# A two-layer gated transformer block in a fixed plan of steps: GpSimd's maxima moved together, turns moved, empty steps put in

## The chip, the core and the metric

The kernel runs on one core of one Trainium2 chip. The metric is the device time of one execution in microseconds (us). Engines: PE (TensorE), DVE (VectorE), ACT (ScalarE), POOL (GpSimd) and SP (SyncE, which issues all DMAs here).

## The reference

Eight batches of 512 tokens with 512 features, a context of 64 rows per batch, four layers one after the other:

```python
x = x + tanh(g_xattn[0]) * linear_attention(layernorm(x), ctx)   # stage A: 16 heads, gate, Wq Wg Wkv Wo
x = x + tanh(g_ffn[0]) * (gelu(layernorm(x) @ W1 + b1) @ W2 + b2)   # stage F: hidden size 2048
x = x + tanh(g_xattn[1]) * softmax(layernorm(x) @ ctx.T, mask) @ ctx
x = x + tanh(g_ffn[1]) * experts(layernorm(x))   # stage E: router over 32, top 8 merged into 8 groups of 192
```

In linear_attention, q and k go through `x + 1 if x > 0 else exp(x)`, and sums of keys times values over the context stand for the scores.

## The kernel before, in words

**Numbers in halves.** Each float32 operand of the large products is scaled by a power of two and split into an f16 "hi" and the f16 rest "lo"; a product is three f16 passes. So every weight tile (128x512) is loaded (SP, L1029), reduced to its largest magnitude by DVE (step `wmax`, L1721), and, once the maximum over a whole matrix is known, split: ACT writes hi (`wsplit`, L1518), DVE writes lo (`wlo`, L1753). The maximum over partitions is POOL's `partition_all_reduce` (step `all`, L1132); `pow` turns it into a scale on DVE (L1659 and after).

**One plan.** `make_plan` writes one list of steps by hand. Each engine walks that list and issues its part of every step in list order, waiting on semaphores; so the list sets the order on each engine, and an engine that waits keeps all later steps of its own back.

**Stage A** (L308 to L452; about 20 to 390 us): keys and values of the context (`kvk`, `kvv`, sums `kvsum`, L1318), then per batch: `q` x4 and `gate` x4 (12 matmuls each, L1259), `numden` x4 (L1327), `att` x4 (a turn, L1278), `out` x4 (L1342). The next batch's x is normalised between them: `stat` (L1686), `rs` (POOL, L1128), `norm` (L1699, two buffers), `turn` (PE transposes into a bank, L1278; ACT copies hi, DVE subtracts lo, L1707). `q` of the next batch needs all four turns. `q` on DVE is L1854, its feature map's sum on POOL L1147; `att` on DVE is L1881, its lo part on POOL L1154 (`attlo`). Beside these, `some()` hands out weight work: one call of `weights` is up to a `wlo`, a `wmax`, a `wsplit` and the `wload`s that are then allowed. The loads have four places in SBUF, tile k takes place k % 4: SP's load of tile k waits until tile k - 4 has left it, by its `wmax` if it was only measured and by its `wlo` if it was split. Every batch ends with a store of x and a load of the next one into the same buffer (SP waits for the store).

**Stage F** (to about 1069 us): `up` and `down` alternate (12 matmuls each, L1259 and L1362). In the last batch the second attention and the router of batch 0 are done between them.

**Stage E** (96 passes s, twelve per batch): PE's steps of a pass are `p16`, `p45`, `p7`, `p23` (12, 12, 6, 12 matmuls of 256 columns, L1269) in banks 4, 5, 4, 6, and four parts of `dn` (3 matmuls, L1460). DVE adds up the banks (L2060; L2065; L2070, L2074; L2081), ACT applies silu, DVE and POOL multiply (`mix`, L2087, L1222), ACT and POOL split the result (`mhi`, L1649, L1228). Between the parts stand five slots per pass, calls of `apart()`: after `p16`, `dn` 0, `dn` 1, `dn` 2, `dn` 3. Each takes one task of `side`, the attention and the router of the batch after (list L, then scores, softmax, reads, list M, then router and gating; all their PE work shares bank 7), and one of `finer`, the last weights. `None` is a task that does nothing. Tasks named below: `scores` (L1377), `soft3` (DVE, L1978 is its last), `pturn`, `read` x4 (L1392; DVE adds to x, L1999), `mturn`, `router` (L1404), `rout4` (L2030), `rout5` (L2035 to L2048), `rturn` (L1413), `gsum` (then SP stores the group weights and loads them for `mix`). The weight forms: `fsplit` (ACT), `flo` (POOL, with four sums that end at L1186), `fhi` (ACT, L1599), `flo2` (POOL, L1191).

Of the kernel before, what the change touches and what calls it, by code (L numbers as in the profile page):

```python
# [14 lines left out]
NT = TOK // P  # L15
NC = D // P
# [50 lines left out]
N_O = 12  # L67
# [66 lines left out]
def make_plan():  # L134
# [119 lines left out]
    def second_tasks(i):  # L254

        ph, b = i

        def stats(ts):
# [17 lines left out]
        if ph == "L":  # L276
            return begin + [norm(0), norm(1), None, turn(0, 2), None, turn(1, 3), None, turn(2), None, turn(3), None]

# [10 lines left out]
        def step(kind):  # L289
            return lambda: add(kind, b)  # L290
        return begin + [norm(0), norm(2), None, turn(0, 1), None, turn(2, 3), None, *s0, turn(1), None, turn(3), None, None,
                        both(lambda: add("router", b, banks=1), s1[0]), both(step("rexp"), s1[1]),
# [77 lines left out]
    for j in range(NC):  # L370
        add("gate", 0, j, banks=1)
        norm()
        if j == 0:
            add("vmax")
            add("all", "v")
        if j == 2:
            add("pow", "v")
        weights(N_O)
    for t in range(4):
        add("kvsum", t, banks=4)  # L380
        if t < 2:
            norm()
    for t in range(NT):
        norm()
        add("numden", 0, t, banks=2)
        weights(N_O)
    add("tables")
    add("all", "b1")
    add("ctxmax")
    add("all", "c")  # L390
    late.append(lambda: add("pow", "c"))
# [12 lines left out]
    for b in range(1, NB):  # L404
        norms = ln_tasks(("A", b + 1) if b + 1 < NB else ("F", 0), apart=True)
        for j in range(NC):
            add("q", b, j, banks=1)
            add("att", b - 1, j, banks=1)
            if j > 0:
                add("attlo", b - 1, j - 1)  # L410
            some()
        for j in range(NC):
            add("gate", b, j, banks=1)
            if j == 0:
                add("attlo", b - 1, NT - 1)
            if b == NB - 1 and j > 0:
                add("numden", b, j - 1, banks=2)
            for _ in range(2 if j < 2 else 1):
                norms.pop(0)()
            some()  # L420
# [43 lines left out]
    def attention_tasks(b):  # L464
# [19 lines left out]
        def gsum():  # L484
            add("gsum", b, banks=1)
            if b == 0:
                add("gload", 0)
                add("gload", 1)
        ahead, one = [None] * (3 if b == 0 else 5 if b == 1 else 0), [None] * (b != 1)
        return [*ahead, *L[:2], split, *L[3:], lambda: add("scores", b, banks=1), None, step("sexp"), step("soft2"),  # L490
                step("soft3"), None, lambda: add("pturn", b, banks=1), None, None, *[read(t) for t in range(NT)], *M,
                *one, lambda: add("rturn", b, banks=1), *one, gsum]

# [51 lines left out]
    def finish_weights():  # L545
# [5 lines left out]
        for t in range(NR):  # L551
            k = (0, 22, 28)[t // 4] + t % 4
            put(k, "wsplit", W_OF["d", t])
            put(k + 1, "wlo", W_OF["d", t])
            if t >= 4:
                put((11, 19)[t // 4 - 1], "wload", W_OF["d", t])
        s0 = W_OF["s", 4 * Q_EARLY]
        for i in range(4):
            put(0 if i < 2 else 5, "wload", s0 + i)
        for i, k in ((0, 12), (2, 16)):  # L560
            put(k, "fsplit", s0 + i)
            put(k + 1, "flo", s0 + i)
            put(k + 1, "fsplit", s0 + i + 1)
            put(k + 2, "flo", s0 + i + 1)
            put(k + 3, "fhi", s0 + i + 1)
            put(k + 4, "flo2", s0 + i + 1)

# [35 lines left out]
    for s in range(total + 3):  # L603
        b, j = divmod(s, NR)
        if s < total:
            if j == 0 and b == 0:
                finer = finish_weights()
            if j == 0 and b + 1 < NB:
                assert not side
                side = attention_tasks(b + 1)  # L610
        if 1 <= s <= total:
# [1527 lines left out]
```

## Time and profile before

| | |
|---|---|
| median of 3 runs | 1862.5 us (1860.62 to 1862.56) |
| profiled execution: its time, its span | 1858.95 us, 1857.2 us |
| mean granted TensorE clock | 0.989 |
| PE busy | 1789.2 us, 96% of the span |
| DVE, ACT, POOL busy | 1152.2, 601.2, 648.1 us |

The span runs from the first to the last instruction; the time has some 1.75 us around it. PE is the engine with almost no idle time, so what is to be read is where its idle time lies, and what ended it.

### The profile page before, as it was taken

How to read it: one execution, taken by the hardware profiler on the slowest of the kernel's cores; microseconds unless marked ns; L12 is line 12 of the kernel's file. 1: busy time of each engine (PE TensorE's matmuls, PEld its weight loads, DVE VectorE, ACT ScalarE, POOL GpSimd, SP SyncE). 2: the span in 40 equal slices, each digit the busy share in tenths (PEclk: the TensorE clock that was granted, in tenths of full speed). 3: DMA queues.
4: the chain of work that ended last, by engine and by line, in shares of the span. 5: the costliest groups of instructions: out<-in, count | busy, mean ns of one | idle time of the engine just before them, and what ended most of it. 6: DMA issues, size and time to landing. Idle time of an engine off the chain costs nothing.

```text
span 1857.2 us, 29113 instructions
## 1 busy us (share of the span) xinstructions
PE 1789.2 (96%) x11224; PEld 1068.4 (58%) x11224; DVE 1152.2 (62%) x2332; ACT 601.2 (32%) x961; POOL 648.1 (35%) x603
## 2 busy tenths in 40 slices
PE   8789999999999999999999979999999999999999
PEld 3545555544444444444444466677777777777776
DVE  5677777754545455453435577868677776768554
ACT  3324534311111124431112354333333434333422
POOL 1122422312012046642010355353544445353633
PEclk9899999999999999999999999999999999999999
DMA  5123443343314223221301051111112121211111
GB/s 160 51 68 123 141 130 103 91 131 67 93 46 114 92 55 97 68 77 34 91 1 63 20 160 57 62 55 54 67 44 77 41 80 41 78 36 54 35 63 46
DMA packets 152620, 137.69 MB, mean 74 GB/s; under 512 B 79970, under 2 KB 96482, under 8 KB 152482
## 3 DMA queue, kind: packets, MB, share of 16 engines
q1 hardware_dynamic: 152482, 135.84, 24.2%
q8 instruction: 88, 1.44, 0.3%
q14 instruction: 50, 0.41, 0.1%
HBM read 103.17 MB, written 32.64 MB: 73 GB/s over the span
## 4 chain that ended last, share of the span: by engine, by line
PE 76%; DVE 11%; POOL 5%; ACT 3%; issue 3%; DMA 2%; SPq 0%; DVEq 0%; ACTq 0%; POOLq 0%
PE bank L1259 21%; PE bank L1269 19%; PE bank L1362 15%; PE bank L1460 10%; PE bank L1342 4%; PE bank L1278 3%; DVE arena L1686 2%; PE bank L1327 1%; PE bank L1308 1%; POOL arena L1216 1%; DVE arena L1753 1%; DVE arena L2087 1%; DVE arena L2081 1%; POOL arena L1222 1%; PE bank L1377 1%
## 5 line engine op out<-in xcount | busy, mean ns | idle before, releaser
L1259 PE MATMUL bank<-arena 128*128 128x512 f16 x2304 | 526.0, 380 | 4.7 <-DVE arena L1707 2.6
L1269 PE MATMUL bank<-arena 128*128 128x256 f16 x4032 | 503.7, 273 | 10.3 <-DVE arena L2060 6.1
L1269 PEld LDWEIGHTS bank<-arena 128*128 128x128 f16 x4032 | 393.0, 98 | 125.8 <-DVE arena L2060 7.6
L1259 PEld LDWEIGHTS bank<-arena 128*128 128x128 f16 x2304 | 225.6, 98 | 269.7 <-issue 3.5
L1362 PE MATMUL bank<-arena 128*128 128x512 f16 x1536 | 356.0, 382 | 3.4 <-DVE arena L1922 2.0
L1460 PE MATMUL bank<-arena 128*128 128x512 f16 x1152 | 310.7, 380 | 0.0
L1912 DVE TENSOR_SCALAR arena<-arena 128x512 f16<-128x512 f32 x128 | 81.6, 637 | 301.2 <-ACT arena L1564 300.8
L1362 PEld LDWEIGHTS bank<-arena 128*128 128x128 f16 x1536 | 150.9, 98 | 186.5 <-issue 4.4
L1564 ACT ACTIVATE arena<-bank,arena 128x512 f32<-128x512 f32 x128 | 99.2, 776 | 429.7 <-PE bank L1259 426.6
L1222 POOL TENSOR_TENSOR arena<-arena 128x512 f32<-128x512 f32 x96 | 121.8, 1269 | 295.9 <-DVE arena L2087 295.9
L1637 ACT ACTIVATE arena<-arena 128x512 f32<-128x512 f32 x96 | 69.3, 722 | 287.8 <-DVE arena L2081 287.7
L1460 PEld LDWEIGHTS bank<-arena 128*128 128x128 f16 x1152 | 112.7, 98 | 58.9 <-issue 0.6
L1128 POOL TENSOR_TENSOR arena<-arena 128x4 f32<-128x4 f32 x32 | 34.4, 1076 | 315.3 <-DVE arena L1691 293.8
L1228 POOL TENSOR_TENSOR arena<-arena 128x512 f16<-128x512 f32 x96 | 113.2, 1179 | 62.1 <-ACT arena L1649 62.1
L1914 DVE SCALAR_TENSOR_TENSOR arena<-arena 128x512 f16<-128x512 f32 x128 | 117.7, 920 | 4.6
L2087 DVE SCALAR_TENSOR_TENSOR arena<-arena 128x512 f32<-128x512 f32 x96 | 74.9, 781 | 54.0 <-ACT arena L1637 53.7
L1147 POOL TENSOR_TENSOR arena<-arena 128x512 f32<-128x512 f32 x32 | 41.9, 1309 | 151.3 <-ACT arena L1540 137.7
L1699 DVE TENSOR_SCALAR arena<-arena 128x512 f32<-128x512 f32 x128 | 81.6, 646 | 18.5 <-POOL arena L1128 18.2
L1278 PE MATMUL bank<-arena 128*128 128x128 f32 x528 | 80.4, 277 | 13.0 <-DVE arena L1699 11.0
L1686 DVE BATCH_NORM_STATS2 arena<-arena 128x6 f32<-128x512 f32 x128 | 85.9, 671 | 8.6 <-DMA arena<-x_after_attention 8.1
L1342 PE MATMUL bank<-arena 128*128 128x512 f16 x384 | 89.1, 384 | 0.0
L2081 DVE TENSOR_TENSOR arena<-bank,arena 128x512 f32<-128x512 f32 x96 | 66.0, 688 | 34.5 <-PE bank L1269 33.8
(188 smaller groups left out, 1841.9 us busy)
## 6 DMA issues: line engine op xcount, KB each, us to landing
arena<-in_L_ffn_proj SPq DMA_DIRECT2D x64, 256.0 KB, 2.7
arena<-group_weights SPq DMA_DIRECT2D x64, 256.0 KB, 3.1
x_after_attention<-arena SPq DMA_DIRECT2D x8, 1024.0 KB, 5.2
arena<-x_after_attention SPq DMA_DIRECT2D x8, 1024.0 KB, 5.6
x_after_ffn<-arena SPq DMA_DIRECT2D x8, 1024.0 KB, 4.3
arena<-x_after_ffn SPq DMA_DIRECT2D x8, 1024.0 KB, 6.5
arena<-group_weights SPq DMA_DIRECT2D x64, 128.0 KB, 2.8
arena<-in_L_ffn_gate_up_proj SPq DMA_DIRECT2D x80, 96.0 KB, 2.0
```

The costliest lines, as they stand in the source:

```text
L1222: e.tensor_tensor(prod_s[s % 2], gw_s[s % 2], prod_s[s % 2], ALU.mult).then_inc(mixed)
L1228: e.tensor_tensor(macth_s[s % 3][1][:, 0, :], prod_s[s % 2], macth_s[s % 3][0][:, 0, :], ALU.subtract).then_inc(m_lo)
L1259: m = e.matmul(bank[b][:, :], wT[l][:, c, tile * P:(tile + 1) * P], y[h][:, c, :], start=n == 0, stop=n == NPASS - 1)
L1269: m = e.matmul(out, forms_of[j // 2][l][:, c, f, (j % 2) * P:(j % 2 + 1) * P], y[h][:, c0 + c, col:col + HT], start=n == 0, stop=n == 2 * ...
L1278: m = e.transpose(block4(b)[:, c, :], src[:, c * P:(c + 1) * P], ident)
L1342: m = e.matmul(bank[k][:, :], aT[h][:, c, cols], woT[l][:, c, :], start=i == 0, stop=i == NPASS - 1)
L1362: m = e.matmul(bank[t][:, :], hv[h][:, 0, t * P:(t + 1) * P], w2T[l][:, j, :], start=j == 0 and i == 0, stop=j == NH - 1 and i == 2)
L1460: m = e.matmul(bank[t][:, :], hv[h][:, 0, t * P:(t + 1) * P], dnT[l][:, j, :], start=j == 0 and i == 0, stop=j == NR - 1 and i == 2)
L1564: e.activation(h_s[(n - 1) % 2], bank[bank_of[step, 0]][:, :], ACT.Gelu, bias=b1T[:, j:j + 1], scale=inv["1"]).then_inc(gelu)
L1686: e.bn_stats(stats[:, t, :], x[:, t, :]).then_inc(bn1)
L1914: e.scalar_tensor_tensor(out=hh[1][:, 0, :], in0=hs, scalar=sc["t1"], in1=hh[0][:, 0, :], op0=ALU.mult, op1=ALU.subtract).then_inc(h_lo)
L2087: e.scalar_tensor_tensor(out=prod_s[s % 2], in0=prod_s[s % 2], scalar=inv["up"], in1=gate_s[s % 2], op0=ALU.mult, op1=ALU.mult).then_inc(prod)
```

## The change

Four things. In stage A, `all` of v, of the context (c) and of b1 stand directly before `all` of o, after batch 1's `rs`; all four turns of batch 1 stand beside the `kvsum`s; `numden` of batch 0 stands after `q` 0 of batch 1, with `pow` v and `tables` there, and batch 0's `att` one step later; the weight tiles of o are split from there on. In stage F's last batch and in stage E the empty tasks are dealt out anew (batch 0: `gap` is empty, 5 ahead; batch 1: 8 ahead; one before read 3, two before `rturn` and one before `gsum` for all). The last weights' times in `finish_weights` are later. `side` may now run over into the next batch.

```diff
@@ second_tasks
+        gap = [None] if b > 0 else []
-            return begin + [norm(0), norm(1), None, turn(0, 2), None, turn(1, 3), None, turn(2), None, turn(3), None]
+            return begin + [norm(0), norm(1), None, turn(0, 2), *gap, turn(1, 3), *gap, turn(2), *gap, turn(3), None]
-        return begin + [norm(0), norm(2), None, turn(0, 1), None, turn(2, 3), None, *s0, turn(1), None, turn(3), None, None,
+        return begin + [norm(0), norm(2), None, turn(0, 1), *gap, turn(2, 3), None, *s0, turn(1), *gap, turn(3), None, None,
@@ make_plan, beside gate of batch 0
         if j == 0:
             add("vmax")
+        if j == 1:
+            add("ctxmax")
+        if j == NC - 1:
             add("all", "v")
-        if j == 2:
-            add("pow", "v")
+            add("all", "c")
+            add("all", "b1")
         weights(N_O)
     for t in range(4):
         add("kvsum", t, banks=4)
-        if t < 2:
-            norm()
-    for t in range(NT):
         norm()
-        add("numden", 0, t, banks=2)
-        weights(N_O)
-    add("tables")
-    add("all", "b1")
-    add("ctxmax")
-    add("all", "c")
+    norm(2)
...
             add("q", b, j, banks=1)
-            add("att", b - 1, j, banks=1)
-            if j > 0:
-                add("attlo", b - 1, j - 1)
+            if b == 1 and j == 0:
+                add("pow", "v")
+                for t in range(NT):
+                    add("numden", 0, t, banks=2)
+                add("tables")
+            if b > 1:
+                add("att", b - 1, j, banks=1)
+                if j > 0:
+                    add("attlo", b - 1, j - 1)
+            elif j > 0:
+                add("att", 0, j - 1, banks=1)
...
@@ attention_tasks
-        ahead, one = [None] * (3 if b == 0 else 5 if b == 1 else 0), [None] * (b != 1)
+        ahead = [None] * (5 if b == 0 else 8 if b == 1 else 0)
-                step("soft3"), None, lambda: add("pturn", b, banks=1), None, None, *[read(t) for t in range(NT)], *M,
-                *one, lambda: add("rturn", b, banks=1), *one, gsum]
+                step("soft3"), None, lambda: add("pturn", b, banks=1), None, None, read(0), read(1), read(2), None, read(3), *M,
+                None, None, lambda: add("rturn", b, banks=1), None, gsum]
@@ finish_weights
-            k = (0, 22, 28)[t // 4] + t % 4
+            k = (8, 27, 33)[t // 4] + t % 4
...
-            put(k + 3, "fhi", s0 + i + 1)
-            put(k + 4, "flo2", s0 + i + 1)
+            put(k + 6, "fhi", s0 + i + 1)
+            put(k + 8, "flo2", s0 + i + 1)
...
-                assert not side
-                side = attention_tasks(b + 1)
+                side += attention_tasks(b + 1)
```

The order on POOL from the feature map of batch 0 (L1147, after the change L1155) to that of batch 1; `ISA` ahead of another kind of instruction is a change of POOL's configuration. Before:

```order
L1147 TENSOR_TENSOR arena<-arena 128x512 x4
L1132 ISA
L1132 ISA arena<-arena 128x1
L1128 ISA
L1128 TENSOR_TENSOR arena<-arena 128x4
L1132 ISA
L1132 ISA arena<-arena 128x1 x3
```

After:

```order
L1155 TENSOR_TENSOR arena<-arena 128x512 x4
L1136 TENSOR_TENSOR arena<-arena 128x4
L1140 ISA
L1140 ISA arena<-arena 128x1 x4
L1155 ISA
L1155 TENSOR_TENSOR arena<-arena 128x512 x3
```

`rs` moved ahead of all maxima, and two of the changes of configuration are gone.

The order on DVE in batch 4 of stage A, from `q` 2: L1854 and L1881 (after the change L1862, L1889) are `q` and `att`, L1753 (L1761) is `wlo`, L1721 (L1729) `wmax`. Before:

```order
L1854 TENSOR_SCALAR arena<-bank 128x512
L1881 SCALAR_TENSOR_TENSOR arena<-arena,bank 128x512
L1753 SCALAR_TENSOR_TENSOR arena<-arena 128x512
L1854 TENSOR_SCALAR arena<-bank 128x512
L1881 SCALAR_TENSOR_TENSOR arena<-arena,bank 128x512
L1753 SCALAR_TENSOR_TENSOR arena<-arena 128x512
L1721 TENSOR_REDUCE arena<-arena 128x1
L1686 BN_STATS arena<-arena 128x6
```

After:

```order
L1761 SCALAR_TENSOR_TENSOR arena<-arena 128x512
L1729 TENSOR_REDUCE arena<-arena 128x1
L1862 TENSOR_SCALAR arena<-bank 128x512
L1889 SCALAR_TENSOR_TENSOR arena<-arena,bank 128x512
L1761 SCALAR_TENSOR_TENSOR arena<-arena 128x512
L1729 TENSOR_REDUCE arena<-arena 128x1
L1694 BN_STATS arena<-arena 128x6
```

Before, the `wlo` ahead of the one `wmax` is of tile 43 and the `wmax` of tile 44; after, the pairs are tiles 40 and 44, 41 and 45, and a third one follows behind the statistics, 42 and 46. The same pairs stand in batch 1 after the change, four of them, tiles 8 and 12 to 11 and 15; before there are none.

The order on DVE at the end of the router's work in stage E, batch 7: L2060, L2065, L2070 (L2068, L2073, L2078) are the sums of `p16`, `p45` and `p7`. Before:

```order
L2060 TENSOR_TENSOR arena<-bank,arena 128x256
L2030 SCALAR_TENSOR_TENSOR arena<-arena 128x128
L2035 TENSOR_REDUCE arena<-arena 128x4
L2037 RECIPROCAL arena<-arena 128x4
L2039 TENSOR_SCALAR arena<-arena 128x4
L2041 TENSOR_TENSOR arena<-arena 128x128
L2046 CAST arena<-arena 128x4x32
L2048 TENSOR_TENSOR arena<-arena 128x4x32
L2065 TENSOR_TENSOR arena<-bank,arena 128x256
L2070 TENSOR_TENSOR arena<-bank,arena 128x256
```

After:

```order
L2038 SCALAR_TENSOR_TENSOR arena<-arena 128x128
L2073 TENSOR_TENSOR arena<-bank,arena 128x256
L2043 TENSOR_REDUCE arena<-arena 128x4
L2045 RECIPROCAL arena<-arena 128x4
L2047 TENSOR_SCALAR arena<-arena 128x4
L2049 TENSOR_TENSOR arena<-arena 128x128
L2054 CAST arena<-arena 128x4x32
L2056 TENSOR_TENSOR arena<-arena 128x4x32
L2078 TENSOR_TENSOR arena<-bank,arena 128x256
```

`rout5` moved from ahead of `p45`'s sum to behind it, ahead of `p7`'s.

## Rows read from the trace of the kernel before

**Rows 1.** Windows: length, busy us (x instructions) by engine, PEclk, DMA share, GB/s.

```profile
989.50:997.20 7.70, 5.19 (x20) 2.47 (x19) 5.23 (x11) 1.37 (x2) 1.44 (x1) 0.78 0.20 51
```

**Rows 2.** PE's waits: us in total, times, longest.

```profile
PE bank L1413 <- DVE arena L2048: 11.3, 8, 2.5
```

**Rows 3.** Timeline of PE, stage A: start, us, what, [idle before <-releaser].

```profile
64.86 3.76 PE L1318 MATMUL bank<-arena 128*128 128x132 f32 x32
71.91 3.86 PE L1318 MATMUL bank<-arena 128*128 128x132 f32 x16 [3.29 <-DVE arena L1841]
...
121.24 1.12 PE L1278 MATMUL bank<-arena 128*128 128x128 f32 x4 [5.68 <-DVE arena L1699]
```

**Rows 4.** Timeline of POOL, stage A.

```profile
67.52 0.38 POOL L1132 PARTITION_ALL_REDUCE arena<-arena  x1 [5.84 <-issue]
...
106.11 1.25 POOL L1147 TENSOR_TENSOR arena<-arena 128x512 f32<-128x512 f32 x1 [6.81 <-issue]
```

**Rows 5.** Timeline of DVE, stage A: one `numden` and `tables`, start to next start.

```profile
83.11 0.35 DVE L1863 TENSOR_SCALAR arena<-bank,arena 128x8 f32<-128x8 f32 x2
...
84.46 0.14 DVE L1659 TENSOR_SCALAR arena<-arena 128x1 uint32<-128x1 uint32 x1
...
94.79 0.42 DVE L1811 CAST arena<-arena 128x512 f32<-128x512 uint8 x1
...
96.51 0.15 DVE L1846 TENSOR_REDUCE arena<-arena 128x1 f32<-128x16 f32 x1
```

**Rows 6.** DMA issues, stage A, two stretches: count, KB each, us to landing.

```profile
arena<-in_L_ffn_proj SPq DMA_DIRECT2D x1, 256.0 KB, 2.9
...
x_after_attention<-arena SPq DMA_DIRECT2D x1, 1024.0 KB, 5.3
```

**Rows 7.** Timeline of DVE, stage A, batch 4.

```profile
229.85 0.74 DVE L1753 SCALAR_TENSOR_TENSOR arena<-arena 128x512 f16<-128x512 f32 x1
...
236.33 1.00 DVE L1699 TENSOR_SCALAR arena<-arena 128x512 f32<-128x512 f32 x2 [0.55 <-POOL arena L1128]
```

**Rows 8.** Timeline of PE, stage A, batch 4.

```profile
237.77 0.60 PE L1278 MATMUL bank<-arena 128*128 128x128 f32 x4
```

**Rows 9.** Timeline of PE, end of stage F.

```profile
992.62 1.12 PE L1278 MATMUL bank<-arena 128*128 128x128 f32 x4 [2.51 <-DVE arena L1699]
...
1005.28 1.56 PE L1377 MATMUL bank<-arena 128*128 128x64 f16 x48 [1.46 <-DVE arena L1707]
...
1046.41 1.41 PE L1404 MATMUL bank<-arena 128*128 128x32 f16 x48 [1.91 <-ACT arena L1564]
...
1058.39 0.38 PE L1413 MATMUL bank<-arena 128*128 128x128 f16 x4 [1.53 <-DVE arena L2048]
```

**Rows 10.** Timeline of DVE, end of stage F.

```profile
1013.67 0.43 DVE L1978 TENSOR_TENSOR arena<-arena 128x256 f16<-128x256 f32 x1
```

**Rows 11.** Timeline of PE, stage E, batch 1's tasks.

```profile
1082.92 1.47 PE L1269 MATMUL bank<-arena 128*128 128x256 f16 x12 [3.07 <-DVE arena L2070]
...
1107.75 0.99 PE L1269 MATMUL bank<-arena 128*128 128x256 f16 x6 [3.73 <-DVE arena L2060]
...
1169.79 0.58 PE L1413 MATMUL bank<-arena 128*128 128x128 f16 x4 [2.51 <-DVE arena L2048]
```

**Rows 12.** Timeline of ACT, stage E.

```profile
1105.82 1.15 ACT L1599 ACTIVATE arena<-arena 128x512 f16<-128x512 f32 x2 [4.93 <-POOL arena L1186]
```

**Rows 13.** Timeline of PE, stage E, batch 2's tasks.

```profile
1218.65 0.39 PE L1392 MATMUL bank<-arena 128*128 128x512 f16 x1 [0.51 <-DVE arena L1999]
...
1262.98 0.38 PE L1413 MATMUL bank<-arena 128*128 128x128 f16 x4 [1.21 <-DVE arena L2048]
```

**Rows 14.** DVE's `rout4`: ns min/median/max; then its timeline at batch 2.

```profile
L2030 DVE SCALAR_TENSOR_TENSOR arena<-arena x8: 284/1240/1243, 1056.3 to 1746.2; 128x128 f32<-128x128 f32 x8
...
1259.11 1.24 DVE L2030 SCALAR_TENSOR_TENSOR arena<-arena 128x128 f32<-128x128 f32 x1
```

**Rows 15.** Timeline of POOL, at the same time.

```profile
1258.93 1.27 POOL L1222 TENSOR_TENSOR arena<-arena 128x512 f32<-128x512 f32 x1 [1.07 <-DVE arena L2087]
```

More of the change, by code:

```diff
@@ L407, in make_plan @@
             add("q", b, j, banks=1)
-            add("att", b - 1, j, banks=1)
-            if j > 0:
-                add("attlo", b - 1, j - 1)
+            if b == 1 and j == 0:
[9 more added lines that the diff above has]
+                add("att", 0, j - 1, banks=1)
+                if j > 1:
+                    add("attlo", 0, j - 2)
             some()
@@ L413, in make_plan @@
             add("gate", b, j, banks=1)
-            if j == 0:
+            if b == 1 and j == 0:
+                add("att", 0, NT - 1, banks=1)
+                add("attlo", 0, NT - 2)
+            if j == (1 if b == 1 else 0):
                 add("attlo", b - 1, NT - 1)
@@ L555, in finish_weights @@
             if t >= 4:
-                put((11, 19)[t // 4 - 1], "wload", W_OF["d", t])
+                put((14, 24)[t // 4 - 1], "wload", W_OF["d", t])
         s0 = W_OF["s", 4 * Q_EARLY]
@@ L559, in finish_weights @@
             put(0 if i < 2 else 5, "wload", s0 + i)
-        for i, k in ((0, 12), (2, 16)):
+        for i, k in ((0, 12), (2, 18)):
             put(k, "fsplit", s0 + i)
```

## The prediction

> **What bounds the kernel now.** I read the page's busy times first: PE works 96% of the span, every other engine under two thirds. So the time is PE's, and a change that leaves the matmuls alone can only move PE's 68 us of idle time and the stretches in which its clock is granted at the lower level. The windows show what a wait costs beyond itself: in the 7.70 us around PE's wait at the end of stage F, PEclk is 0.78 [rows 1], so (1 − 0.78) × 7.70 = 1.7 us are lost to the clock after 2.51 us of waiting. I charge this 1.7 us only where a wait is over 2.5 us. Then PE's waits, by what ended them: a group that this change aims at is `rturn` waiting for the router on DVE, 11.3 us in eight waits [rows 2]. Last the timelines of PE and of the engine that it waited for, at each place that the change reaches. What matters there is not the engine's load but which step stands last in its row ahead of the one that PE wants.
>
> **Start of stage A, a gain of 3.8 us.** The sums of keys and values (`kvsum`) run 32 matmuls in 3.76 us at first, and behind a wait of 3.29 us for DVE only 16 in 3.86 us: the lower clock [rows 3]. The cause behind it is POOL: each change of its configuration costs it some six to seven us in which it does nothing that PE could use, 5.84 us ahead of the maximum of v and 6.81 us ahead of the feature map [rows 4]. After the change `rs` of batch 1 runs first, then all maxima, and two of these changes are gone. So norm and turns stand ready earlier: from 64.86, 64 matmuls at 3.76/32 us are 7.5 us, four turns 1.8 (estimate: one is 0.60 us [rows 8] and overlaps its neighbour by some 0.16), waits for the later turns' banks some 3.6 (estimate: before, turns at that place waited for the same chain of DVE and ACT), and `q` 0, 12 matmuls of 512 columns, 2.7 (twice the 1.47 us of 12 with 256 columns, less the ends that overlap [rows 11]): it ends near 80.5.
>
> From there DVE has a serial row that PE needs: the reduction of a maximum 0.6, four `numden` of 1.35 (83.11 to 84.46), `tables` 1.72 (94.79 to 96.51) [rows 5], three `pow` at some 0.7 each (estimate: four instructions like the 0.14 one, start to start). That is 0.6 + 5.4 + 1.7 + 2.1 = 9.8, some 90.5 to 91 us. Then four times `q` and `att` and each time the weights' pair `wlo`, `wmax`. All four work on 128x512 as the `wlo` of 0.74 us in [rows 7] does, and I take 0.6 to 0.7 for each from start to start: 1.2 and 1.3 a pair.
>
> Here is a cost that the change doesn't name. The tiles of such a pair are k and k + 4, so they share a place: SP may issue the load of k + 4 only when `wlo` of k has ended, and the `wmax` next in DVE's row needs that load. A load of 256 KB takes 2.9 us [rows 6]. Four pairs: 4 × (1.2 + 1.3 + 2.9) = 21.6 us, to 112.5; the statistics of batch 2 add 3.2 (four of 0.8, estimate by the same row), `rs` and the first norm 1.3 (0.55 and half of 1.00 [rows 7], and the passing on): the turn of batch 2 comes near 117.4. PE, meanwhile, has from 80.5 seven groups (18.4 us), `numden` 3.6 and turns 1.8, is done at 104.3, and waits some 13 us. In before that turn comes at 121.24 after 5.68 us [rows 3]. So 3.8 us are gained. Lower bound 2 (one more load in the row), upper bound 5 (the loads land while POOL's feature map holds DVE up anyway).
>
> **Stage A, batch 4, a loss of 9.7 us.** The same hazard stands in the row of DVE that is quoted above: three pairs on one place (40 and 44, 41 and 45, 42 and 46) where before only tiles 43 and 44 stood together, on different places. Before, DVE begins the `wlo` of 43 at 229.85 and the norm of batch 5 at 236.33 [rows 7]; the turn that needs it runs at 237.77 without any wait [rows 8]. After, 3 × 2.95 us of waiting for loads (2.9 and the semaphore) and 1.3 us for one more `wlo` and `wmax` are added; DVE has some 1.6 us of gaps that soak part of it up, 0.55 of it ahead of the norm [rows 7]. The norm then starts at 236.33 + 8.85 + 1.3 − 1.6 = 244.9, the turn at 245.4: PE waits 7.6 us, and the clock adds 2. Bounds: nothing, if the loads turn out to be issued earlier or later than I read it; 12 if nothing is soaked up. At the ends of batches 1 and 4 one load, of tile 22 and tile 54, is queued on SP behind the store of x, which takes 5.3 us [rows 6], and the load of x behind it. DVE stands there about 4.65 us; most of that falls where DVE was waiting for PE anyway, so I put 0.6 us each on PE's path, 1.2 together. Stage A behind its start so loses 10.9 us.
>
> **End of stage F, a gain of 1.1 us.** Four waits stand here: 2.51 before a turn, 1.46 before `scores`, 1.91 before `router`, 1.53 before `rturn` [rows 9]. With five empty tasks ahead, the turn has its norm earlier (0.8 left), and the two tasks before `rturn` take its wait away. But the empty tasks were taken out from between other steps. Softmax runs from the end of `scores` (1005.28 + 1.56 = 1006.84) to 1014.10 [rows 10], 7.3 us, and the matmuls now standing between `scores` and `pturn` are worth only 5.2: a new wait of about 2.2. Router 2.4 instead of 1.91, and `gsum`, now close behind `rturn`, 0.8. 7.4 before against 6.3 after: 1.1 us.
>
> **Stage E, tasks of batch 1, a gain of 4.5 us.** Before, PE waits 3.07 and 3.73 us for DVE's sums and 2.51 before `rturn`, with the clock down twice [rows 11]. The second begins with ACT, which stands 4.93 us for POOL's sums of the last weights (`flo`) [rows 12]; with `fhi` three and `flo2` four slots later nothing queues behind them. That removes 3.73 + 2.51 + 1.7 = 7.9 us. Against it: the splits of the `d` tiles move from slots 0 to 4 into 8 to 12, where the statistics of the next batch are, and I expect three waits of 2 to 3 us there instead of the 3.07 and its neighbours, 3.4 us more. Net 4.5; bounds 0 and 8.
>
> **Stage E, batches 2 to 7, a gain of 8 us.** Each batch has a wait of 0.51 before read 3, and at `rturn` 1.21 (batch 2) [rows 13]; the other five are alike, since (11.3 − 1.53 − 2.51)/6 = 1.21 [rows 2, 9, 11]. An empty task ahead of each gives one part of `dn` more, over 1 us of matmuls. 6 × 1.72 = 10.3 us. Against it: `rout5` now stands between the sums of `p45` and `p7`, and `side` spills by up to six tasks into the next batch, which shifts the phases of batches 2 to 4. I take 2.3 us off. One row says that `rout5`'s place may matter: `rout4` takes 1.24 us in most batches and 0.28 at best, and at batch 2 its 1.24 us [rows 14] lie inside the 1.27 us of POOL's multiplication that began at 1258.93 [rows 15]. So DVE was held there. By the Trainium skill, "SBUF — State Buffer", section "SBUF: two separate sides", a DVE operation with two operands in SBUF and a GpSimd operation exclude each other from a shared pair of ports for a whole instruction; the trace agrees in this place. By that rule `rout5`'s two multiplications could each lose 1 us if `mix` on POOL falls upon them, and `p7`'s sum would then reach PE up to 0.6 us late per batch, 3.6 us in all; the sum goes by the 2.3 us.
>
> **The sum.** −3.8 + 10.9 − 1.1 − 4.5 − 8.0 = −6.5 us. The profiled execution took 1858.95 us with a span of 1857.2; so 1850.7 and 1852.5. The median of the runs shown, 1862.5, lies 3.6 above it: 1856.0.
>
> **The rivals.** 0.2% of this kernel, about what a measurement can tell from no change, is 3.7 us.
>
> *DVE's waits in batch 4 do not reach PE.* For it: DVE has slack on average there. Against it: the turn at 237.77 follows the norm at 236.33 by 1.4 us, so there is no slack for 8.85. If half of it is hidden and the boundary costs nothing, the loss is 1 to 2: about 1847. Chance 0.2.
>
> *The empty tasks only move waits in stages F and E.* A fixed number of slots holds more tasks, and each task taken out from between two others makes a new wait; in batch 1 three in place of three. Then stages F and E give 9.5 of the 13.6, or less, and the time is 1860.5, within 0.2%. Chance 0.25.
>
> *Slower: the loads that stand one place too near in DVE's row.* Nothing is soaked up in batch 4 (3 × 2.95 + 1.3 − 0.8 = 9.3) and the waits at the two batch ends reach PE with 3.75 each, and each of the three brings the lower clock (1.5 each): 9.3 + 7.5 + 4.5 = 21 in place of 10.9: 1866. It decides from a DVE wait of 4 us or more at either batch end that falls ahead of a norm. Chance 0.1.
>
> **How the numbers follow.** The forecast has 0.45, and takes 1852 to 1860 from the bounds of stage A's start (2 to 5) and of stage E (±3.5). The range 1848 to 1862.5 leaves out the far half of the first rival and the slower one. Faster by over 0.2% (below 1858.8): 0.4 of the forecast's 0.45, the 0.2, and 0.03 of the second; 0.63. Within: 0.26. Slower (over 1866.2): 0.11, with mishaps in stage E.
>
> **What will show it.** In the timeline of PE: the turn of batch 2 near 117 with a wait of some 13 us; a turn of batch 4's successor near 241 (245.4 less the start's gain) with a wait of 7 to 8 us. In that of DVE: `wmax` waiting for a DMA of W in batches 1 and 4, some 2.9 us each. In PE's waits: `rturn`'s row near zero, the one before read 3 gone, a new one before `pturn` at the end of stage F. On POOL: two gaps of 6 to 7 us fewer before 110 us. I am wrong if DVE shows no such waits (then nearer 1847), or if the sums L2060 to L2081 make PE wait by more than 5 us more in stage E than before (then no gain).

## The result and the profile after

The changed kernel is slower: 1877.36 us (median of four runs) against 1861.56, a ratio of 1.0093 with a 95% interval of 1.0077 to 1.0109. The profiled execution spans 1873.6 us instead of 1857.2, 16.4 more. The forecast was 1856.0. One execution of all those below, of the kernel b1_before, took 2329.33 us and stands in no ratio.

To find the place I read both timelines of PE at the same matmul. Between two marks PE has the same work in both kernels, but for a few matmuls of tasks that moved across a mark, so the difference at a mark is what was lost up to there. (Where stage E is cut into twelve passes, the mark is the first matmul of `p16` of the batch's first pass.)

(The forecast's 8.0 us for batches 2 to 7 are split evenly.)

| stretch | before | after | difference | forecast |
|---|---|---|---|---|
| up to `q` 0 of batch 2 | 138.95 | 137.78 | −1.2 | −3.8 |
| from `q` 0 of batch 4 to that of batch 5 | 38.17 | 50.46 | +12.3 | +9.7 |
| all up to the first `down` (about stage A's end) | 390.36 | 402.15 | +11.8 | +7.1 |
| stage F | 678.82 | 675.48 | −3.3 | −1.1 |
| stage E, first 12 passes (batch 1's tasks) | 105.93 | 107.48 | +1.6 | −4.5 |
| passes with the tasks of batches 2, 3, 4 | 97.4 each | 103.79, 98.75, 101.72 | +12.0 | −4 |
| passes with the tasks of batches 5, 6, 7 | 97.4 each | 95.6 each | −5.5 | −4 |

Below are the windows of the changed kernel for these stretches: the start and batch 4 of stage A, then stage E with the tasks of batches 1 to 5. Columns: length, busy us of PE, PEld, DVE, ACT, POOL, PEclk, DMA share, GB/s.

```profile
50.46:137.78 87.32, 67.84 (x370) 40.70 (x370) 60.11 (x151) 24.33 (x40) 18.59 (x18) 0.86 0.13 44
214.27:264.73 50.46, 40.51 (x211) 22.35 (x208) 31.84 (x65) 15.50 (x25) 11.45 (x9) 0.90 0.34 110
1077.63:1185.11 107.48, 91.20 (x753) 67.76 (x752) 80.93 (x157) 50.28 (x86) 58.30 (x54) 0.97 0.30 91
1185.11:1288.90 103.79, 97.92 (x794) 71.12 (x795) 72.35 (x155) 35.37 (x58) 45.85 (x40) 0.98 0.17 56
1288.90:1387.65 98.75, 95.48 (x799) 70.84 (x797) 74.58 (x162) 36.38 (x59) 46.05 (x41) 1.00 0.19 58
1387.65:1489.37 101.72, 95.70 (x798) 70.65 (x796) 75.10 (x158) 36.26 (x59) 46.02 (x40) 1.00 0.18 57
1489.37:1584.95 95.58, 95.01 (x794) 70.76 (x793) 70.90 (x156) 36.66 (x60) 47.20 (x40) 1.00 0.20 61
```

The last row is what an undisturbed batch now takes: PE is busy for 95.01 of 95.58 us. Three batches before it, with the same instructions, take 3.2 to 8.2 us more. So the loss has two places, stage A's batch 4 and the first batches of stage E.

In stage A the timeline of PE shows the turn of batch 2 (which answers to the last row of [rows 3]) and that of batch 5 (which answers to [rows 8], where there was no wait):

```profile
119.26 1.11 PE L1286 MATMUL bank<-arena 128*128 128x128 f32 x4 [14.03 <-DVE arena L1707]
...
246.86 1.11 PE L1286 MATMUL bank<-arena 128*128 128x128 f32 x4 [9.96 <-DVE arena L1707]
```

Both wait for the norm (L1707). DVE's waits between 80 and 260 us (total, times, longest) say why the norm is late; in the kernel before, this stretch has no wait of that kind:

```profile
DVE arena L1729 <- DMA arena<-in_L_ffn_proj: 25.4, 9, 4.3
DVE arena L1862 <- PE bank L1267: 12.7, 10, 4.3
```

and the timeline of DVE in batch 4 shows where they stand, between a `wlo` (L1761) and the `wmax` (L1729) behind it:

```profile
225.36 1.75 DVE L1761 SCALAR_TENSOR_TENSOR arena<-arena 128x512 f16<-128x512 f32 x1
231.45 0.69 DVE L1729 TENSOR_REDUCE arena<-arena 128x1 f32<-128x512 f32 x1 [4.34 <-DMA arena<-in_L_ffn_proj]
...
233.24 0.74 DVE L1761 SCALAR_TENSOR_TENSOR arena<-arena 128x512 f16<-128x512 f32 x1
236.66 0.69 DVE L1729 TENSOR_REDUCE arena<-arena 128x1 f32<-128x512 f32 x1 [2.67 <-DMA arena<-in_L_ffn_proj]
```

In stage E no single wait explains the loss. The overrun of `side` is 6 tasks when batch 2's begin, 4 for batch 3, 2 for batch 4 (58 tasks in 60 slots gain two back each time). At the first of these, four engines hang in one chain. In order: the timelines of POOL, ACT, DVE and PE of the changed kernel near 1205 us.

```profile
1201.96 1.27 POOL L1230 TENSOR_TENSOR arena<-arena 128x512 f32<-128x512 f32 x1 [12.84 <-DMA arena<-group_weights]
```

```profile
1203.26 0.63 ACT L1657 ACTIVATE arena<-arena 128x512 f16<-128x512 f32 x1 [6.62 <-POOL arena L1230]
...
1204.41 0.49 ACT L1581 ACTIVATE arena<-arena 128x256 f16<-128x256 f32 x1
```

```profile
1204.94 0.93 DVE L1938 SCALAR_TENSOR_TENSOR arena<-arena 64x512 f16<-64x512 f32 x1 [3.59 <-ACT arena L1581]
```

```profile
1207.37 0.65 PE L1286 MATMUL bank<-arena 128*128 128x128 f32 x4 [1.71 <-DVE arena L1707]
```

The router weights of batch 1 are written by its last task, `gsum`, which is now six slots late; POOL's multiplication of the pass stands for them (12.84 us), ACT's split of its result stands for POOL, the context's split (L1581) behind it is late, DVE's lo part of the context (L1938) waits for that, the norm stands behind it, and PE's turn waits for the norm. In batch 4 no group weights are late, and yet 6.1 us are lost. The wait of 2.67 us that ends at the mark 1185.11 is counted with batch 1's passes.

### The profile page after: what moved, and what is told of

Read it like the earlier page. It is cut to its first block, busy times and chain, and to the rows that moved or that the text cites. A ratio compares the mean times of both kernels' runs of the same rounds, so it can differ in the third digit from the quotient of the medians.

```text
span 1873.6 us, 29111 instructions
## 1 busy us (share of the span) xinstructions
PE 1787.2 (95%) x11224; PEld 1063.8 (57%) x11224; DVE 1162.1 (62%) x2332; ACT 596.8 (32%) x961; POOL 652.0 (35%) x603
## 4 chain that ended last, share of the span: by engine, by line
PE 74%; DVE 12%; issue 4%; POOL 3%; DMA 3%; ACT 3%; SPq 0%; DVEq 0%; POOLq 0%; ACTq 0%
PE bank L1267 20%; PE bank L1277 17%; PE bank L1370 16%; PE bank L1468 9%; PE bank L1350 5%; PE bank L1286 2%; DVE arena L1694 2%; DMA arena<-in_L_ffn_proj 1%; PE bank L1335 1%; DVE arena L1761 1%; PE bank L1316 1%; DVE arena L1707 1%; POOL arena L1230 1%; DVE arena L2089 1%; PE bank L1385 1%
## 5 line engine op out<-in xcount | busy, mean ns | idle before, releaser
L1236 POOL TENSOR_TENSOR arena<-arena 128x512 f16<-128x512 f32 x96 | 112.9, 1176 | 66.1 <-ACT arena L1657 66.1
L1155 POOL TENSOR_TENSOR arena<-arena 128x512 f32<-128x512 f32 x32 | 41.0, 1280 | 179.5 <-ACT arena L1548 172.2
L1286 PEld LDWEIGHTS bank<-arena 128*128 128x128 f32 x528 | 63.2, 142 | 61.8 <-DVE arena L1707 35.1
L1707 DVE TENSOR_SCALAR arena<-arena 128x512 f32<-128x512 f32 x128 | 83.9, 659 | 17.0 <-POOL arena L1136 16.3
L1657 ACT ACTIVATE arena<-arena 128x512 f16<-128x512 f32 x96 | 60.1, 626 | 106.2 <-POOL arena L1230 106.0
```

Source lines behind the costliest of these rows:

```text
L1236: e.tensor_tensor(macth_s[s % 3][1][:, 0, :], prod_s[s % 2], macth_s[s % 3][0][:, 0, :], ALU.subtract).then_inc(m_lo)
L1286: m = e.transpose(block4(b)[:, c, :], src[:, c * P:(c + 1) * P], ident)
L1707: e.tensor_scalar(yn_s[(n - 1) % 2], x[:, t, :], mv[:, t, 0:1], rs[:, t:t + 1], ALU.subtract, ALU.mult).then_inc(yn_ok)
```

## The experiments

Most change a few words of the plan. Times are medians unless one run is named; "before" was measured beside them (1858.6 to 1859.5 us).

**1. `wmax` held back (hold).** The maximum of a tile is left for a later call of `weights` while the `wlo` that freed its place is among the last five steps.

```diff
@@ weights
-        if pre[0] < min(upto, load[0]):
+        if pre[0] < min(upto, load[0]) and ("wlo", pre[0] - 4) not in P_.steps[-5:]:
```

> The changed kernel, but the maximum of a weight tile (k + 4) is not taken directly behind the splitting of tile k that frees its place: `weights` holds it back to its next call. Theory (a DVE wait for a load stands ahead of the norm): the DVE waits of 2.6 to 4.3 us in batches 1 and 4 of stage A are gone, the turn of batch 2 comes some 9 us earlier than at 119.26 and that of batch 5 without a wait of 9.96, and stage F begins some 17 to 21 us earlier than at 402.15 (12.3 of batch 4, 5 to 9 of batch 1). Rival (PE's 14 us wait at the start is the serial row of numden, pow and tables on DVE and the feature map on POOL, and the loads fall beside it): only the 12.3 us of batch 4 come back, and the turn stays within 2 us of 119.26.

1857.38 us, ratio to before 0.9985 (0.9976 to 0.9995); 20 us less than the changed kernel. The first `down` comes at 382.56 us, 19.6 earlier than in the changed kernel (17 to 21 were expected) and 7.8 earlier than before. The timeline of PE at the turns of batches 2 and 5:

```profile
113.72 1.11 PE L1286 MATMUL bank<-arena 128*128 128x128 f32 x4 [6.90 <-DVE arena L1707]
...
230.26 0.66 PE L1286 MATMUL bank<-arena 128*128 128x128 f32 x4
```

DVE's waits for a weight tile in the same stretch:

```profile
DVE arena L1729 <- DMA arena<-in_L_ffn_proj: 0.9, 1, 0.9
```

25.4 us became 0.9, with no fewer loads issued in this stretch (45, in the changed kernel 42). The turn of batch 2 came 5.5 us earlier, not 9: a wait of 6.90 us stays there. The place of one small reduction in DVE's row made the loss of stage A. The rival, that the loads fell beside other waits of DVE, is out: of the 19.6 us, 6.9 came back by `q` 0 of batch 2 and 11.9 more by that of batch 5.

**2. No overrun (ahead2).**

```diff
@@ attention_tasks
-        ahead = [None] * (5 if b == 0 else 8 if b == 1 else 0)
+        ahead = [None] * (5 if b == 0 else 2 if b == 1 else 0)
```

> The changed kernel, with 2 empty tasks ahead of batch 1's attention instead of 8, so that its 60 tasks fill the 60 slots and none runs over into batch 2. Theory (the overrun of 6, 4 and 2 slots puts the steps of batches 2, 3 and 4 beside other parts of a pass, and that makes the new waits): each of the batches 2 to 4 of stage E becomes as short as the batches 5 to 7 (from mark to mark 95.6 us instead of 103.8, 98.8 and 101.7), 17 us in all; batch 1's own waits get worse by up to 4 us; time 1862 to 1866. Rival (the router's later steps between the sums of p45 and p7, with POOL holding DVE, make them): the waits in batches 2 to 4 stay, time 1875 to 1880.

1874.94 us. The windows of stage E with the tasks of batches 1 to 4:

```profile
1080.10:1204.08 123.98, 97.44 (x758) 70.92 (x757) 80.92 (x164) 49.92 (x85) 59.23 (x54) 0.92 0.26 78
1204.08:1299.66 95.58, 95.02 (x794) 70.80 (x793) 70.87 (x156) 36.66 (x60) 47.16 (x40) 1.00 0.21 61
...
1395.24:1490.82 95.58, 95.01 (x794) 70.77 (x793) 71.11 (x156) 36.10 (x59) 47.19 (x40) 1.00 0.19 60
```

The half on batches 2 to 4 held to a tenth of a us: 95.58 each, 17.5 us back. With that the rival is out, since `rout5` stands where it stood. The half on batch 1 was wrong by far: not up to 4 us but 16.5 more, 123.98 instead of 107.48, and 6.2 of them are PE's own work at the lower clock (busy 97.44 us, PEclk 0.92, instead of 91.20 and 0.97). So the time expected, 1862 to 1866, was missed; against the changed kernel the 2.4 us less are not clear of the scatter, since the intervals overlap (1.0061 to 1.0096 here, 1.0077 to 1.0109 there). PE's waits in its passes are led by these:

```profile
PE bank L1277 <- DVE arena L2078: 9.1, 4, 5.6
PE bank L1394 <- DVE arena L1986: 5.7, 1, 5.7
PE bank L1286 <- ACT arena L1619: 4.1, 1, 4.1
```

A wait of 5.7 us before `pturn`, where the changed kernel has 2.4. I argue that with two tasks ahead, the statistics, softmax and second turns of batch 1 lie upon the last weights, which begin at slot 8; no run moves them alone. Two empty tasks ahead are too few, then, but eight are not needed: experiments 5 and 6 have five and no overrun.

**3. The last weights at their old times (fwold).** `finish_weights` as before, all else changed.

> The changed kernel with the last weights' times of before (splits from slot 0, fhi three and flo2 four slots behind). Theory (the splits of slots 8 to 12 crowd DVE and ACT just where the statistics and norms of batch 1's attention stand): the waits between 1089 and 1105 us, 7.3 us in all, fall to some 3, the one of 3 to 5 us for POOL's sums comes back near slot 15, and stage E's first 12 passes are shorter by 0 to 3 us. Rival (the overrun and the 8 empty tasks make them): the waits of 2.97, 1.79 and 1.56 stay, and a fourth one is added, 3 us longer.

One run, 1873.02 us. The first twelve passes take 106.5 us instead of 107.5, the next 102.1 instead of 103.8. The waits between 1089 and 1105 us fell to 3.2 (2.31 and 0.85), as expected, and the wait for POOL's sums came back, as expected too: 3.65 us, which PE now spends before `scores`. In order: ACT, DVE and PE of this run.

```profile
1113.53 1.15 ACT L1607 ACTIVATE arena<-arena 128x512 f16<-128x512 f32 x2 [3.35 <-POOL arena L1194]
```

```profile
1114.98 0.42 DVE L2068 TENSOR_TENSOR arena<-bank,arena 128x256 f32<-128x256 f32 x1 [3.67 <-ACT arena L1640]
```

```profile
1116.22 2.74 PE L1385 MATMUL bank<-arena 128*128 128x64 f16 x48 [3.65 <-DVE arena L1715]
```

`fhi` on ACT (L1607) stands for POOL's sums, ACT's step behind it (L1640) is late, the sum of `p16` on DVE waits for that, and the lo part of a turn (L1715) that `scores` wants stands behind the sum. So the later times take one wait of 3.65 us away and put 4.1 us between 1089 and 1105 in its place. What is left is 1 us in batch 1's passes, which is no more than profiles of equal steps differ there (below).

**4. Both repairs (hold_ahead2).**

> Both of the edits above in the changed kernel. If the two causes are separate the gains add up: 1877.4 - 17 to 21 - 12 to 16, so 1842 to 1849, and the kernel before is beaten by 0.7 to 1%. If either theory falls, 1858 to 1866.

1853.87 us, 0.9971 (0.9959 to 0.9984): the expected 1842 to 1849 is missed. What ahead2's edit gives is small with `wmax` held back as without (1857.38 − 1853.87 = 3.5 beside 1877.36 − 1874.94 = 2.4), because batch 1 keeps its loss: 120.7 us for its passes. That the two edits leave each other's gain alone is in line with this, and no more.

**5 and 6. Batch 1 as before (b1_before, b1_list).** `one` is a list that is empty for batch 1 alone; 59 tasks, 58 for the others, no overrun. b1_before has the old times of the last weights too, b1_list the changed ones.

```diff
@@ attention_tasks
-        ahead = [None] * (5 if b == 0 else 8 if b == 1 else 0)
+        ahead, one = [None] * (5 if b < 2 else 0), [None] * (b != 1)
...
-                step("soft3"), None, lambda: add("pturn", b, banks=1), None, None, read(0), read(1), read(2), None, read(3), *M,
-                None, None, lambda: add("rturn", b, banks=1), None, gsum]
+                step("soft3"), None, lambda: add("pturn", b, banks=1), None, None, read(0), read(1), read(2), *one, read(3), *M,
+                *one, *one, lambda: add("rturn", b, banks=1), *one, gsum]
```

> The changed kernel with `wmax` held back, batch 1's tasks of stage E and the last weights' times as before (5 ahead, 59 tasks), and the changed list for batch 0 and the batches 2 to 7. Theory (the three causes are separate: loads in stage A, batch 1's own crowding, the overrun): stage F ends near 1060, batch 1's twelve passes take 106 us as before, each later batch 95.6: 1839, between 1836 and 1842. Rival (part of the waits is made by the changed batches themselves and was hidden by the others' lateness): 1848 or more.

> As the kernel beside it, but with the changed times of the last weights (splits from slot 8, fhi six and flo2 eight slots behind). Tells whether these times alone help batch 1: if what stands before POOL's sums costs PE 3.7 us and no new wait comes, 3 to 5 us faster than its neighbour; if the splits in slots 8 to 12 crowd DVE and ACT beside the norms, 3 to 10 us slower. With 2 tasks ahead batch 1 lost 15 us against before, so I expect the second.

1838.85 us, 0.9889 (0.9869 to 0.9909), and 1837.82 us, 0.9886 (0.9869 to 0.9902). The first met its expectation of 1839 closely; the second missed mine, which was 3 to 10 us slower than its neighbour: they are equal, 106.60 and 106.33 us for the first twelve passes. The windows of b1_list with the tasks of batches 1 and 2:

```profile
1057.49:1163.82 106.33, 91.08 (x758) 67.36 (x757) 81.97 (x164) 50.66 (x86) 58.80 (x54) 0.98 0.31 93
1163.82:1259.40 95.58, 95.01 (x795) 70.76 (x793) 71.09 (x156) 36.11 (x59) 47.20 (x40) 1.00 0.20 60
```

This version beats the kernel before by 1.1%, and the changed one by 39.5 us.

**7. A whole pass of overrun (ahead7).** `hold` with `7 if b == 1`; the overrun is 5, 3 and 1 tasks.

> The changed kernel with `wmax` held back and 7 empty tasks ahead of batch 1 instead of 8: the overrun is 5, 3 and 1 tasks instead of 6, 4 and 2. Five tasks are a whole pass. Theory (what matters is beside which part of a pass a step stands): batch 2 is now as short as without any overrun, 95.6 us and not 103.9, while the batches 3 and 4 have waits in new places, 1 to 6 us each. Rival (any overrun is late for batch 2, so its waits grow with it): batch 2 takes 100 us or more, batches 3 and 4 less than with 4 and 2 (98.8 and 103.4).

1850.33 us, 0.9949 (0.9932 to 0.9966). Batches 2, 3, 4 take 97.4, 99.2 and 98.0 us; with 6, 4 and 2 (hold) they take 103.9, 98.8 and 103.4. So batch 2, late by nearly as much, is short again when the lateness is a whole pass. The 1.8 us above 95.6 I put down to the group weights, still late, in the timeline of POOL:

```profile
1185.75 1.27 POOL L1230 TENSOR_TENSOR arena<-arena 128x512 f32<-128x512 f32 x1 [8.16 <-DMA arena<-group_weights]
```

POOL stands 8.16 us here and 12.74 in hold. One task less makes 6.5 us for batch 2, and both the place and the lateness of the weights changed with it, so this run alone doesn't part them. Batches 3 and 4, with overruns of 3 and 1, stand 3.6 and 2.4 us above 95.6, as expected. Batch 1's own passes took 111.42 us, in hold 107.73: one empty task fewer was no help there.

**8. The place without the lateness (phase).** b1_list with `{5: 2, 6: 1}.get(b, 0)` empty tasks ahead from batch 2 on: nothing runs over.

> The kernel with both repairs (b1_list) and 2 empty tasks more ahead of batch 5's work, 1 more ahead of batch 6's: 60 and 59 tasks in 60 slots, nothing runs over, and the group weights are asked for in time. Their work is done in the fifth and sixth batch of passes of stage E. Theory (the place in the pass alone makes the waits, without any lateness): the fifth takes some 102 us (as batch 4 did in the changed kernel with an overrun of 2: 101.7) and the sixth some 98 (as with an overrun of 1: 98.0), the others 95.6. Rival (it was the group weights that came late after an overrun): both stay at 95.6.

One run, 1848.9 us. The windows of the fifth to seventh batch of passes of stage E, and the timeline of PE in the fifth:

```profile
1452.87:1556.08 103.21, 97.16 (x794) 71.20 (x793) 74.08 (x156) 35.71 (x58) 46.06 (x40) 0.98 0.17 56
1556.08:1654.07 97.99, 95.70 (x794) 70.50 (x793) 72.66 (x156) 36.69 (x60) 46.55 (x40) 1.00 0.19 59
1654.07:1749.63 95.56, 95.00 (x794) 70.81 (x793) 71.06 (x156) 36.11 (x59) 47.21 (x40) 1.00 0.13 45
```

```profile
1465.81 0.83 PE L1277 MATMUL bank<-arena 128*128 128x256 f16 x6 [1.69 <-DVE arena L2068]
...
1491.29 0.38 PE L1394 MATMUL bank<-arena 128*128 128x128 f16 x4 [0.29 <-DVE arena L1986]
...
1498.54 0.39 PE L1400 MATMUL bank<-arena 128*128 128x512 f16 x1 [1.21 <-DVE arena L2007]
...
1532.73 0.63 PE L1286 MATMUL bank<-arena 128*128 128x128 f32 x4 [2.72 <-ACT arena L1619]
```

The changed kernel has, in batch 4, the same four waits: 1.69 before `p7`, 0.29 before `pturn`, 1.21 before a read, 2.69 before a turn. 98.0 is also what ahead7 measured for an overrun of one. So two tasks more ahead of a batch cost 7.6 us and one costs 2.4, with no lateness at all: it is the place in the pass. Of the 7.6 us, 1.5 are the clock, which fell behind the wait of 2.72 us here and not in the changed kernel, where batch 4 lost 6.1.

This settles batches 3 and 4, not the whole of batch 2. Its overrun of 6 is a pass and one slot, and one slot alone costs 2.4 us, with waits of 1.07 before a turn, 0.51 before a read, 0.20 before a `p16` and 0.38 before the router. The changed kernel has these in batch 2 as well (1.90, 0.52, 0.20, 0.38); the other 5.8 of its 8.2 us go with the chain from the late group weights that is shown above and with a low clock at the batch's start. No run takes the lateness away and leaves the slot.

The largest of them, read on PE's releasers in the changed kernel: first ACT, then POOL.

```profile
1466.95 0.60 ACT L1619 ACTIVATE arena<-bank 128x512 f32<-128x512 f32 x1 [3.24 <-POOL arena L1224]
```

```profile
1463.17 1.16 POOL L1236 TENSOR_TENSOR arena<-arena 128x512 f16<-128x512 f32 x1 [1.69 <-ACT arena L1657]
1464.29 2.57 POOL L1224 TENSOR_TENSOR arena<-arena 128x1024 f16<-128x1024 f32 x1
```

`mturn`'s copy on ACT (L1619) needs the buffer that POOL's long subtraction (L1224, 2.57 us) reads; that one stands on POOL behind the split of the pass's product (L1236), which has a fixed place in the pass. In a batch without a shift the order on POOL at this place is the other one, here from batch 5 of the changed kernel:

```profile
1557.55 2.13 POOL L1224 TENSOR_TENSOR arena<-arena 128x1024 f16<-128x1024 f32 x1
1561.11 1.16 POOL L1207 TENSOR_TENSOR arena<-arena 128x512 f16<-128x512 f32 x1 [1.43 <-ACT arena L1622]
1562.23 1.15 POOL L1236 TENSOR_TENSOR arena<-arena 128x512 f16<-128x512 f32 x1
```

Two slots later, the long subtraction falls behind the split instead of ahead of it, and PE waits 2.69 us for the next turn.

**9 and 10. Each half alone (a_hold, e_only).** The kernel before with the changed stage A and `wmax` held back, and the kernel before with the changed stages F and E of b1_list.

> The kernel before with the changed stage A alone, `wmax` held back; stages F and E as before. Theory (stage A's part is worth 7.8 us by itself once no DVE wait for a load stands ahead of a norm, nothing of it is given back later): stage F begins at 382.6 instead of 390.4 and the time is 7.8 us under before, 1851. Rival (part of it is owed to the other edits, or lost again in stage F, where the weight loads stand otherwise): 1855 to 1859.

> The kernel before with the changed tasks of stages F and E alone, batch 1 as before (5 ahead, 59 tasks, no overrun); stage A as before. Theory (the empty tasks save 1.85 us in each of six batches if nothing runs over, and the end of stage F 1 to 3 us): 1859 - 11 - 2 = 1846, between 1844 and 1848. With a_hold's gain it should add up to what the kernel with both measured, 1837.8.

1852.06 us, 0.9957 (0.9940 to 0.9974), and 1848.14 us, 0.9939 (0.9923 to 0.9956): 7.4 and 11.3 us under before, 18.7 together; the kernel with both has 20.8. The sum is 2 us short, within the scatter. a_hold is 1 us over its expectation: stage A brings 7.1 (first `down` at 383.30), but its first twelve passes of stage E take 108.99 us where before, with the same steps, they take 105.93. e_only lies at the upper edge of its range, and all six of its batches take 95.6 us; its stage A, the same as before, ends 1.7 us later. Differences under 3 us in those passes, and under 2 in stage A, are therefore not told from one profile.

## Why the prediction was wrong

Forecast and profile lie 22.9 us apart (−6.5 and +16.4). Batches 2 to 7 of stage E make 14.5 of them, batch 1 of stage E 6.1, stage A 4.7, and stage F takes 2.2 off (each rounded).

**Stage E, batches 2 to 7: the step that failed.** It took 10.3 us for the empty tasks and took 2.3 off for the overrun and for `rout5`. The first term was right: six batches without a shift save 1.85 us each, 11.1 in all (b1_list). The second was mis-sized by 15 us: against 95.58 us a batch, the overrun costs 8.2 + 3.2 + 6.1 = 17.5. The wait of 2.67 us at the end of batch 1's passes belongs to it too: it stands there with an overrun of 6 (also in hold and fwold), is 0.70 with one of 5 (ahead7) and absent with none (ahead2, b1_list). I treated a shift as a scatter of small waits, while tasks and passes fit together like a comb: in a batch of 60 slots, one or two slots move every step of the side work against the fixed sums, splits and multiplications of the pass (phase: 2.4 and 7.6 us). The text gave the overrun ("up to six tasks") and its batches, and then put a number on it that no row stood behind. My sign of being wrong did not fire either: the sums on DVE made PE wait 13.0 us instead of 10.3, under the 5 more that I named, and the gain was gone all the same, since most of the new waits stood before turns, reads and `pturn`.

**Stage E, batch 1: no gain.** The forecast was 4.5 us of gain; +1.6 was measured, which one profile does not tell from nothing. The waits that I took away did go: the 3.73 for POOL's sums (fwold brings it back as 3.65) and `rturn`'s 2.51 [rows 11]. But the clock fell twice as before, and the term against them, put at 3.4 us, came out at 6.0: waits of 2.97, 1.79, 1.56, 2.41 and 1.46 us stand there now with some small ones, 13.6 in all, where 7.6 would have been left. The one of 2.67 for POOL, which is the overrun's, comes on top. The rival "three in place of three" describes it, and mildly. That the last weights' times bring nothing by themselves is shown by b1_list beside b1_before.

**Batch 4 of stage A: right in mechanism, 2.6 us too small.** Three waits of DVE of 4.34, 2.67 and 2.59 us stood for 3 × 2.95, and the `wlo` ahead of the first took 1.75 us instead of some 0.74; PE waited 9.96 us instead of 7.6, and 4.32 us of what followed ran at the lower clock, 2.2 us lost against the 2 that I charged. The first wait is the one that I had at 2.95; that load was issued beside batch 6's x (1024 KB), which I argue lengthened it but did not test. The two batch ends, forecast at 1.2 us together, cost 0.7 (DVE waits of 3.31 and 3.45 us instead of 4.65). The clock was of the right size here: from the end of the wait on only the rest of the low stretch counts.

**Start of stage A: −1.2 for −3.8.** The turn came at 119.26 instead of 117.4. The loads took what was forecast (3.02, 2.78, 2.67 and 2.77 us); DVE's row ahead of them ended at 92.58, not at 90.5 to 91: `q` 0 of batch 1 ran partly at the lower clock, took 4.23 us instead of 2.7 and ended at 81.75, not 80.5, and a `numden` took 1.54 us from start to start instead of 1.35. The rest, some 0.8 us, is the clock: PE ran its next 5.63 us at half speed after the turn, 2.8 us lost, against 2 at that turn before. The unhindered gain is 8.0 us up to `q` 0 of batch 2 (hold, 130.93 instead of 138.95): the change's idea was worth twice my figure, and the hazard ate nearly all. On POOL two of four gaps are gone, as forecast (5.84, 7.03, 6.03 and 6.81 us before; 6.09 and one inside a wait of 11.57 for ACT after); what of the 8.0 us is theirs and what the moved turns', no run tells.

**End of stage F: right in the waits.** The waits were forecast as 0.8, 0, 2.2, 2.4, 0 and 0.8, and are these in the changed kernel's timeline:

```profile
1003.99 1.11 PE L1286 MATMUL bank<-arena 128*128 128x128 f32 x8 [0.50 <-DVE arena L1707]
```

then 2.13 before `pturn`, 2.71 before `router`, 0.97 before `gsum`, 6.3 in all, as forecast. The stage gained 3.3 and not 1.1 because PE's own work in it took 2.65 us less: the clock was low for 3.41 us three times before and once after. One of the two that are gone stood at the turn's wait of 2.51 [rows 9]. The other stood at 807.91 behind a wait of 2.03 us that no edit touches, and the changed kernel has one of 1.79 in that part without a low stretch. That part of the gain is luck; other runs with the changed steps take 675.1 to 677.2 us for the stage.

**`rout5` and the shared port.** The estimate by the Trainium skill ("SBUF — State Buffer", section "SBUF: two separate sides") of 0.6 us per batch did not come: in batches 5 to 7 nothing waits for `rout5`. The trace agrees with the rule and puts the sign the other way: the new place is the faster one. `rout5`'s first multiplication, ns min/median/max, in the changed kernel:

```profile
L2049 DVE TENSOR_TENSOR arena<-arena x8: 291/293/1127, 1064.6 to 1767.2; 128x128 f32<-128x128 f32 x8
```

Before (L2041) the median was 1124 ns: it used to lie upon POOL's split of the product (at batch 2, DVE 1261.12 to 1262.24, POOL's L1228 1260.94 to 1262.10), and behind `p45`'s sum it comes after it (at batch 7, DVE from 1767.20, POOL's split until 1767.14).

**The rivals.** The slower one had 0.1, and would have been 1866 from stage A alone. Its mechanism was the right one for the first loss, but its condition was a wait of 4 us or more at a batch end, where 3.31 and 3.45 us were measured; I had no case in which stage A's loss met a loss in stage E, which is what happened. Together they gave 11.8 in stage A and 8.0 in stage E, less 3.3 in stage F.

**Slips in the sums.** The turn of batch 2 follows from the terms as given at some 117.0, not 117.4, and the waits at the end of stage F add up to 6.2, not 6.3. Neither matters beside the rest.

## What to carry to other kernels

A step that needs a transfer which the step just ahead of it on the same engine sets free costs the whole transfer (2.6 to 4.3 us each here); look for such pairs in the order after every change of the pacing, and keep one step of distance (19.6 us here for one condition).

When side work runs beside a loop with a fixed number of slots, count tasks against slots, and treat a shift as a new schedule: measure each offset, or pad so that the batches begin in phase. A fix for one batch must not leave an offset for the next.

## What was not expected of the hardware

The granted clock fell for 17.07 us about the 14.03 us wait of PE (107.82 to 124.89), for 10.24 us about the 9.96 us wait, and for 6.83 us about the waits of 5.68 us (before) and 6.90 us (hold). The two long ones reach 5.6 and 4.3 us past the end of the wait, and this part alone costs time. Windows of the changed kernel from the end of each wait to the end of the stretch:

```profile
119.26:124.89 5.63, 5.63 (x16) 2.54 (x17) 3.08 (x8) 0.60 (x1) 0.00 (x0) 0.50 0.52 175
246.86:251.18 4.32, 4.32 (x13) 2.05 (x14) 2.79 (x5) 0.60 (x1) 0.00 (x0) 0.50 0.92 286
```

So after a wait of 14 us the price was 2.8 us and after one of 10 us 2.2. Read in the same way, the wait of 2.51 us in [rows 1] cost 1.5, not the 1.7 of the prediction, which took in a part inside the wait. In the kernel before, from its end on:

```profile
992.62:995.64 3.02, 3.02 (x9) 1.60 (x10) 2.69 (x5) 0.60 (x1) 0.00 (x0) 0.50 0.51 130
```

Nor does a short wait have a fixed price. Behind the same turn, after 2.72 us of waiting in phase the clock was low, and after 2.69 us in the changed kernel it was not:

```profile
1533.33:1536.74 3.41, 3.41 (x16) 2.00 (x14) 0.85 (x2) 1.94 (x4) 3.41 (x3) 0.50 0.00 0
```

```profile
1467.69:1471.00 3.31, 3.31 (x27) 2.62 (x28) 0.88 (x3) 2.21 (x5) 2.71 (x3) 1.00 0.00 0
```
